# The silu-up product kept in the PSUM bank of up: a mixture-of-experts feed-forward with a mask product on VectorE

## The chip, the cores and the metric

The kernel runs on one core of a Trainium2 chip. The metric is the device time of one execution in microseconds. The engines are named TensorE (PE), VectorE (DVE), ScalarE (ACT), GpSimd (POOL) and SyncE (SP); PEld is TensorE's weight load.

## What is computed

Two layers of a gated transformer run one after the other on x, 4 sequences of 512 tokens with 128 features (2048 tokens in all). Each layer adds a gated cross-attention term (in layer 0 an alignment by dynamic time warping, in layer 1 an attention with 16 heads) and then a gated feed-forward term. The change touches only the feed-forwards. Cut to what matters, they are

```python
# layer 0: 64 experts of width 64, the 8 best by sigmoid score; one shared expert
expert_act = silu(gate_out) * up_out                       # per token and expert
routed = einsum(expert_act * router_mask[..., None], expert_down_k)
# layer 1: 8 experts of width 344, the 2 best by softmax; one shared expert
y = y + cw[:, e:e+1] * (silu(xf @ wg[e].T) * (xf @ wu[e].T)) @ wd[e].T
```

All experts are computed for all tokens; the routing weight, zero where a token did not choose the expert, is multiplied in as a mask before the down projection.

## The kernel before, in words

Tokens stand in the free dimension: xn_hi and xn_lo hold the normalised x transposed, 128 features by 2048 tokens, split into a rounded high part and the low rest, because TensorE multiplies in a reduced fp32 format. A product of two split operands takes three matmuls (`three_pass`, L1010 to L1014: high by high, low by high, high by low).

The hidden units of all experts, the shared one included, are cut into groups of 128: 33 groups in feed-forward 0 and 25 in feed-forward 1. The 2048 tokens are cut into four chunks of 512. A **unit** is one group on one chunk, u = 4g + k; there are 132 and 100 of them, 232 in all. Per unit:

- TensorE, `gate_up` (L1128 to L1139): three matmuls of 512 columns for gate into PSUM bank 4 + k % 2, three for up into bank 6 + k % 2. Then `down` (L1141 to L1148) of unit u - 2: two matmuls with the high part of the masked product (L1144, L1145), and a third (L1147), which waits for its low part. They add up in banks 0 to 3, one per chunk, over all groups.
- ScalarE, `unit` (L836 to L848): act_s = silu(gate) (L846); then `hi` (L829 to L834) of unit u - 1, which rounds act_a to act_hi.
- VectorE, `unit` (L1629 to L1648): L1639 multiplies act_s by the up bank into act_t, L1647 multiplies act_t by the mask into act_a.
- GpSimd, `unit` (L695 to L701): L700 subtracts, act_lo = act_a - act_hi.
- Once per group, at chunk 2, ScalarE rounds the next group's weights (L842) and VectorE computes their low part (L1626), 128 by 384 each, both in SBUF.
- SyncE's queue reloads a half of the weight buffer (L477, L480; L489 in feed-forward 1) when the group that used it is done with it, and a half of the mask buffer (L486; L500), a megabyte per group written to 128 partitions, when `act` says that the last product of the group two before is through.

Every tile between the engines has two halves, taken in turn by k % 2, and each step waits on counting semaphores: `gate`, `up`, `silu`, `t` (L1639 done), `act` (L1647 done), `ahi`, `alo`, `down`. Each engine works through its list in order. The waits that the change touches are on TensorE, before the gate of unit u:

```python
pe.wait_ge(FF[f]["silu"], u - 1)
pe.wait_ge(FF[f]["t"], u - 1)
```

A wait for the value u - 1 means that unit u - 2 has passed that step. ScalarE also waits for `t` of u - 2 before it writes act_s again.

The first 3 groups and the last 2 are written out; between them runs a hardware loop on each engine over 4 groups (16 units) per turn, 7 turns in feed-forward 0 and 5 in feed-forward 1. In the first units of feed-forward 0, VectorE also does the top-8 routing, in those of feed-forward 1 the top-2 routing, each step placed by hand in front of a unit (`ROUTE1_BEFORE`). After the last unit the sums are copied to yT, transposed back into banks 4 to 7 and added to x (`close`, `back`, `add_ffn`).

SBUF tiles of stages that do not overlap share one `arena`; the trace shows mask, act_s, act_t, act_a, yT and xT all by that name, and every PSUM bank as `bank`.

Of the kernel before, what the change touches and what calls it, by code (L numbers as in the profile page):

```python
# [29 lines left out]
P = 128  # L30
# [6 lines left out]
def program(nc, x, ctx_1024, g_xattn, g_ffn, r0_w, sg0, su0, sd0, eg0, eu0, ed0,  # L37
# [23 lines left out]
    CHUNKS = TOK // 512  # L61
# [17 lines left out]
    FT = -(-FLAT // P)  # L79
# [18 lines left out]
    with ctx:  # L98
# [6 lines left out]
        ps = [ctx.enter_context(nc.psum_tensor(f"bank{i}", [P, 512], F32)) for i in range(8)]  # L105
# [69 lines left out]
        mark = [0]  # L175
# [46 lines left out]
        mark[0] = 0  # L222
        mask = view([2, TOK])
        act_s = view([2, 512])
        act_t = view([2, 512])
        act_a = view([2, 512])
        yT = view([CHUNKS, 512])
        mark[0] += FT * P
        XT_FROM = mark[0]
        xT = view([TOK])  # L230
        aff = [view([TILES, E]) for E in EXPERTS]
# [699 lines left out]
        def _(pe):  # L931
# [52 lines left out]
            for g in range(GROUPS[1]):  # L984
                j = g % 2
# [24 lines left out]
            def three_pass(out, w_h, w_l, x_h, x_l, start=True, stop=True):  # L1010

                nc.tensor.matmul(out, w_h, x_h, start=start, stop=False)  # L1012
                nc.tensor.matmul(out, w_l, x_h, start=False, stop=False)  # L1013
                return nc.tensor.matmul(out, w_h, x_l, start=False, stop=stop)  # L1014
# [110 lines left out]
            def feed_forward(f):  # L1125
                units = CHUNKS * GROUPS[f]

                def gate_up(g, k, j):  # L1128
                    u = CHUNKS * g + k
                    if k == 0:  # L1130
                        pe.wait_ge(FF[f]["wlo"], g + 1)
                    if not (isinstance(g, int) and u < 2):
                        pe.wait_ge(FF[f]["silu"], u - 1)
                        pe.wait_ge(FF[f]["t"], u - 1)
                    tok = slice(512 * k, 512 * (k + 1))
                    three_pass(ps[4 + k % 2][:], w_hi[:, j, 0:P], w_lo[:, j, 0:P],
                               xn_hi[:, tok], xn_lo[:, tok]).then_inc(FF[f]["gate"], 1)
                    three_pass(ps[6 + k % 2][:], w_hi[:, j, UP:UP + P], w_lo[:, j, UP:UP + P],
                               xn_hi[:, tok], xn_lo[:, tok]).then_inc(FF[f]["up"], 1)  # L1139

# [30 lines left out]
                for n in range(CHUNKS):  # L1171

                    nc.tensor.matmul(ps[n][:], zeros[0:1, 0:P], zeros[0:1, :], start=True, stop=False)
                for u in range(2, CHUNKS * PEEL):
                    gate_up(u // CHUNKS, u % CHUNKS, u // CHUNKS % 2)
                    down(u - 2, (u - 2) % CHUNKS, (u - 2) // CHUNKS % 2)
                with pe.Fori(0, LOOPS[f]) as t:
# [13 lines left out]
                def back(n):  # L1191

                    if n == 0:
                        pe.wait_ge(FF[f]["silu"], units)
                    if n == 2:
                        pe.wait_ge(FF[f]["t"], units)
                    pe.wait_ge(FF[f]["yT"], n + 1)
                    for q in range(4):
                        mm = nc.tensor.transpose(ps[4 + n][:, P * q:P * (q + 1)], yT[:, n, P * q:P * (q + 1)], ident[:])
                    mm.then_inc(FF[f]["back"], 1)  # L1200
# [18 lines left out]
        def _(dve):  # L1219
# [402 lines left out]
            def feed_forward(f):  # L1622
# [6 lines left out]
                def unit(g, k, j, half, last=False):  # L1629
# [4 lines left out]
                        split_lo(g + 1, 1 - j)  # L1634
                    dve.wait_ge(FF[f]["silu"], u + 1)
                    dve.wait_ge(FF[f]["up"], u + 1)
                    if not early:
                        dve.wait_ge(FF[f]["act"], u - 1)
                    nc.vector.tensor_tensor(act_t[:, i, :], act_s[:, i, :], ps[6 + i][:], ALU.mult).then_inc(FF[f]["t"], 1)  # L1639
                    if f == 0 and isinstance(g, int) and g == 1:  # L1640
                        dve.wait_ge(s_mask1[k], 16 * MASK_DMAS)
                    elif k == 0:
# [1 line left out]
                    dve.wait_ge(FF[f]["t"], u + 1)  # L1644
                    if not early:
                        dve.wait_ge(FF[f]["alo"], u - 1)
                    nc.vector.tensor_tensor(act_a[:, i, :], act_t[:, i, :], mask[:, j, 512 * k:512 * (k + 1)],  # L1647
                                            ALU.mult).then_inc(FF[f]["act"], 1)  # L1648

                for g in range(PEEL):  # L1650
# [57 lines left out]
```

## Time and profile before

| | |
|---|---|
| runs (us) | 926.32, 926.35, 929.34; median 926.35 |
| profiled execution: span from first to last instruction (us) | 928.2 |
| profiled execution: own time | not listed apart from the runs |
| instructions | 13152 |
| busy, share of the span | PE 77%, VectorE 83%, ScalarE 47%, GpSimd 47% |
| mean granted TensorE clock | 0.868 of full |
| feed-forward 0, first gate after the opening to the last unit's gate (us) | 228.3 to 535.7 |
| feed-forward 1, the same (us) | 680.9 to 912.8 |

The span and the runs are measured in different executions. Busy time is the time in which an engine had an instruction under way; matmuls are pipelined, so one takes about 0.40 us while the next starts 0.23 us after it. The number behind an idle time in a row is what ended it. Instructions that wait for a port or a buffer inside the engine are shown as longer, not as idle.

### The profile page before, as it was taken

To read this page: it belongs to the slowest core of one execution; us is meant where nothing else is said; L and a number is where in the kernel's file an instruction comes from. 1 tells how busy PE (TensorE), PEld (TensorE's weight loads), DVE (VectorE), ACT (ScalarE), POOL (GpSimd) and SP (SyncE) were. 2 spreads that over 40 slices of the span, in tenths; PEclk is the share of its full clock that TensorE was granted. 3 is DMA by queue.
4 is the path that set the end of the run, shared out by engine and by line. 5 is a ranking of instruction groups with operands and counts; after the bars stand their busy time and mean duration, and the time that the engine had idled before them with its cause. 6 is when DMAs were issued, how large, how long until landed. Compare 5 with 4: busy or idle time off the path is not lost.

```text
span 928.2 us, 13152 instructions
## 1 busy us (share of the span) xinstructions
PE 714.0 (77%) x3115; PEld 537.3 (58%) x3115; DVE 773.9 (83%) x1829; ACT 432.5 (47%) x757; POOL 438.0 (47%) x451
## 2 busy tenths in 40 slices
PE   3422200038999999999999978999999999999996
PEld 2211100036776676767667647998866767766674
DVE  6599569998899898989889887777697988989895
ACT  2344100024555555555555545444445555555553
POOL 5568600005655556565555652110136565555653
PEclk9655555555999999999999978999589999999999
DMA  4454650003676675757666400000327656455551
GB/s 122 78 127 137 146 65 0 0 9 75 147 146 124 131 137 124 140 113 146 121 136 132 116 1 9 1 0 0 72 53 147 145 114 147 117 142 127 129 131 46
DMA packets 84164, 89.44 MB, mean 96 GB/s; under 512 B 48958, under 2 KB 61859, under 8 KB 80609
## 3 DMA queue, kind: packets, MB, share of 16 engines
q1 hardware_dynamic: 79808, 79.38, 41.3%
q0 software_dynamic: 4320, 9.68, 3.7%
q8 instruction: 11, 0.18, 0.1%
q14 instruction: 25, 0.20, 0.1%
HBM read 79.84 MB, written 8.70 MB: 95 GB/s over the span
## 4 chain that ended last, share of the span: by engine, by line
DVE 27%; issue 27%; PE 25%; POOL 11%; ACT 5%; DMA 3%; SPq 1%; POOLq 1%; DVEq 0%
POOL act_lo L700 10%; DVE arena L1647 8%; DVE junk L1417 6%; PE bank L1012 4%; PE bank L1076 4%; PE bank L1014 4%; PE bank L1013 4%; ACT act_hi L834 3%; PE bank L1147 2%; PE bank L1058 2%; DVE arena L1374 2%; DVE arena L1383 1%; PE bank L948 1%; DVE arena L1639 1%; PE bank L1144 1%
## 5 line engine op out<-in xcount | busy, mean ns | idle before, releaser
L700 POOL TENSOR_TENSOR act_lo<-arena,act_hi 128x512 fp32r<-128x512 f32 x232 | 323.4, 1403 | 237.7 <-ACT act_hi L834 232.1
L1647 DVE TENSOR_TENSOR arena<-arena 128x512 f32<-128x512 f32 x232 | 311.2, 1341 | 22.1 <-POOL act_lo L700 12.3
L846 ACT ACTIVATE arena<-bank 128x512 f32<-128x512 f32 x232 | 138.9, 599 | 140.7 <-PE bank L1014 137.2
L834 ACT ACTIVATE act_hi<-arena 128x512 fp32r<-128x512 f32 x232 | 147.0, 633 | 94.2 <-PE bank L1147 51.0
L1012 PE MATMUL bank<-xn_hi,w_hi 128*128 128x512 f32 x464 | 188.4, 406 | 3.1 <-issue 1.9
L1639 DVE TENSOR_TENSOR arena<-arena,bank 128x512 f32<-128x512 f32 x232 | 157.8, 680 | 37.1 <-ACT arena L846 19.6
L1013 PE MATMUL bank<-xn_hi,w_lo 128*128 128x512 f32 x464 | 185.6, 400 | 0.0
L1014 PE MATMUL bank<-xn_lo,w_hi 128*128 128x512 f32 x464 | 185.6, 400 | 0.0
L1147 PE MATMUL bank<-act_lo,w_hi 128*128 128x512 f32 x232 | 104.1, 449 | 31.2 <-POOL act_lo L700 30.9
L1012 PEld LDWEIGHTS bank<-xn_hi,w_hi 128*128 128x128 f32 x464 | 88.7, 191 | 26.8 <-issue 7.2
L1014 PEld LDWEIGHTS bank<-xn_lo,w_hi 128*128 128x128 f32 x464 | 88.5, 191 | 21.1
L1013 PEld LDWEIGHTS bank<-xn_hi,w_lo 128*128 128x128 f32 x464 | 88.5, 191 | 18.9
L1144 PE MATMUL bank<-act_hi,w_hi 128*128 128x512 f32 x232 | 92.6, 399 | 0.0
L1145 PE MATMUL bank<-act_hi,w_lo 128*128 128x512 f32 x232 | 91.8, 396 | 0.0
L1147 PEld LDWEIGHTS bank<-act_lo,w_hi 128*128 128x128 f32 x232 | 43.6, 188 | 83.2 <-POOL act_lo L700 77.8
L602 POOL TENSOR_SCALAR xn<-x_res,mv,rstd 128x128 f32<-128x128 f32 x16 | 13.8, 866 | 135.9 <-DVE rstd L1307 106.8
L992 PE MATMUL bank<-ident,prep_in 128*128 128x128 f32 x75 | 22.1, 431 | 64.8 <-DMA prep_in<-in_L_ffn_wd 57.7
L1417 DVE TENSOR_SCALAR_CACHE_REDUCE junk<-arena,ecol 4x511 f16<-4x511 f16 x76 | 56.5, 744 | 8.3 <-DMA arena<-arena 5.6
L1000 PE MATMUL bank<-ident,ecol 128*77 128x128 f32 x1 | 0.5, 499 | 77.7 <-DVE junk L1417 77.7
L992 PEld LDWEIGHTS bank<-ident,prep_in 128*128 128x128 f32 x75 | 12.4, 210 | 74.3 <-DMA prep_in<-in_L_ffn_wd 69.5
L1144 PEld LDWEIGHTS bank<-act_hi,w_hi 128*128 128x128 f32 x232 | 43.6, 188 | 11.4 <-issue 0.7
L1145 PEld LDWEIGHTS bank<-act_hi,w_lo 128*128 128x128 f32 x232 | 43.8, 189 | 10.2
(199 smaller groups left out, 956.2 us busy)
## 6 DMA issues: line engine op xcount, KB each, us to landing
arena<-scr_mask SPq DMA_DIRECT2D x94, 512.0 KB, 6.2
scr_w<-prep_out POOLq DMA_DIRECT2D x25, 192.0 KB, 2.2
w_raw<-scr_w SPq DMA_DIRECT2D x25, 192.0 KB, 6.5
arena<-scr_one SPq DMA_DIRECT2D x6, 512.0 KB, 6.0
w_raw<-in_L_ffn_expert_gate_k SPq DMA_DIRECT2D x32, 64.0 KB, 6.1
w_raw<-in_L_ffn_expert_up_k SPq DMA_DIRECT2D x32, 64.0 KB, 5.8
w_raw<-in_L_ffn_expert_down_k SPq DMA_DIRECT2D x64, 32.0 KB, 5.4
prep_in<-in_L_ffn_wg POOLq DMA_DIRECT2D x21, 64.0 KB, 2.4
```

Of the source, the lines that this page charges most:

```text
L700: nc.gpsimd.tensor_tensor(act_lo[:, k % 2, :], act_a[:, k % 2, :], act_hi[:, k % 2, :].bitcast(F32), ALU.subtract).then_inc(FF[f]["alo"], 1)
L834: nc.scalar.activation(act_hi[:, j, :], act_a[:, j, :], ACT.Copy).then_inc(FF[f]["ahi"], 1)
L846: nc.scalar.activation(act_s[:, k % 2, :], ps[4 + k % 2][:], ACT.Silu).then_inc(FF[f]["silu"], 1)
L1012: nc.tensor.matmul(out, w_h, x_h, start=start, stop=False)
L1013: nc.tensor.matmul(out, w_l, x_h, start=False, stop=False)
L1014: return nc.tensor.matmul(out, w_h, x_l, start=False, stop=stop)
L1144: nc.tensor.matmul(ps[n][:], w_hi[:, j, DOWN:DOWN + P], act_hi[:, i, :], start=False, stop=False)
L1145: nc.tensor.matmul(ps[n][:], w_lo[:, j, DOWN:DOWN + P], act_hi[:, i, :], start=False, stop=False)
L1147: nc.tensor.matmul(ps[n][:], w_hi[:, j, DOWN:DOWN + P], act_lo[:, i, :], start=False, stop=False).then_inc(FF[f]["down"], 1)
L1417: nc.vector.tensor_scalar(junk[CHASE, 1:S], chase[:, i, 1:S], ecol[CHASE, i:i + 1], 0.0, ALU.is_le, ALU.add, accum_out=ecol[CHASE, i - 1:i ...
L1639: nc.vector.tensor_tensor(act_t[:, i, :], act_s[:, i, :], ps[6 + i][:], ALU.mult).then_inc(FF[f]["t"], 1)
L1647: nc.vector.tensor_tensor(act_a[:, i, :], act_t[:, i, :], mask[:, j, 512 * k:512 * (k + 1)], ALU.mult).then_inc(FF[f]["act"], 1)
```

## The change

L1639 writes its product back into the PSUM bank that it reads up from, and L1647 reads it there. The tile act_t goes; the arena's later views keep their addresses from xT on, and act_a and yT move down. Since the bank of up is now in use until the mask product is done, TensorE's wait moves: before the gate it waits for `silu` only, and before up for `act` of unit u - 2 instead of `t`. VectorE's wait for its own `act` before L1639 goes. Units 2 and 3, which have none of these waits to stand for it, get a wait on xn_lo of their chunk (`wait_low`). The transposes at the end into bank 6 wait for the last `act` instead of the last `t`.

```diff
         act_s = view([2, 512])
-        act_t = view([2, 512])
         act_a = view([2, 512])
         yT = view([CHUNKS, 512])
-        mark[0] += FT * P
+        mark[0] += FT * P + 2 * 512
@@ TensorE, gate_up
                     if not (isinstance(g, int) and u < 2):
                         pe.wait_ge(FF[f]["silu"], u - 1)
-                        pe.wait_ge(FF[f]["t"], u - 1)
                     tok = slice(512 * k, 512 * (k + 1))
                     three_pass(ps[4 + k % 2][:], w_hi[:, j, 0:P], w_lo[:, j, 0:P],
                                xn_hi[:, tok], xn_lo[:, tok]).then_inc(FF[f]["gate"], 1)
+                    if not (isinstance(g, int) and u < 2):
+                        pe.wait_ge(FF[f]["act"], u - 1)
                     three_pass(ps[6 + k % 2][:], w_hi[:, j, UP:UP + P], w_lo[:, j, UP:UP + P],
                                xn_hi[:, tok], xn_lo[:, tok]).then_inc(FF[f]["up"], 1)
@@ TensorE, feed_forward
                 for u in range(2, CHUNKS * PEEL):
+                    if u < CHUNKS:
+                        wait_low(pe, 2 * f + 1, u)
                     gate_up(u // CHUNKS, u % CHUNKS, u // CHUNKS % 2)
@@ TensorE, back
                     if n == 2:
-                        pe.wait_ge(FF[f]["t"], units)
+                        pe.wait_ge(FF[f]["act"], units)
@@ VectorE, unit
                     dve.wait_ge(FF[f]["up"], u + 1)
-                    if not early:
-                        dve.wait_ge(FF[f]["act"], u - 1)
-                    nc.vector.tensor_tensor(act_t[:, i, :], act_s[:, i, :], ps[6 + i][:], ALU.mult).then_inc(FF[f]["t"], 1)
+                    nc.vector.tensor_tensor(ps[6 + i][:], act_s[:, i, :], ps[6 + i][:], ALU.mult).then_inc(FF[f]["t"], 1)
...
-                    nc.vector.tensor_tensor(act_a[:, i, :], act_t[:, i, :], mask[:, j, 512 * k:512 * (k + 1)],
+                    nc.vector.tensor_tensor(act_a[:, i, :], ps[6 + i][:], mask[:, j, 512 * k:512 * (k + 1)],
                                             ALU.mult).then_inc(FF[f]["act"], 1)
```

## Rows read from the trace of the kernel before

**Rows 1.** Costliest groups: line, engine, operation, count | busy us, mean ns | idle before, releaser

```profile
L1647 DVE TENSOR_TENSOR arena<-arena 128x512 f32<-128x512 f32 x232 | 311.2, 1341 | 22.1 <-POOL act_lo L700 12.3
```

**Rows 2.** Timeline in the loop of feed-forward 0: start us, duration us, engine, line

```profile
343.47 1.29 POOL L700 TENSOR_TENSOR act_lo<-arena,act_hi 128x512 fp32r<-128x512 f32 x1 [1.37 <-ACT act_hi L834]
...
343.61 1.71 DVE L1647 TENSOR_TENSOR arena<-arena 128x512 f32<-128x512 f32 x1
...
348.53 0.69 DVE L1647 TENSOR_TENSOR arena<-arena 128x512 f32<-128x512 f32 x1
```

**Rows 3.** Windows: stretch, length, busy PE, PEld, DVE, ACT, POOL, clock, DMA, GB/s

```profile
263.90:529.30 265.40, 249.70 (x1006) 184.36 (x1005) 238.31 (x252) 149.75 (x251) 154.59 (x112) 1.00 0.65 132
709.00:905.00 196.00, 184.40 (x745) 136.62 (x744) 176.33 (x186) 111.21 (x186) 114.12 (x83) 1.00 0.58 132
```

**Rows 4.** Waits in 263.9 to 529.3: total us, times, longest us

```profile
PE bank L1147 <- POOL act_lo L700: 14.6, 28, 0.6
```

**Rows 5.** Timeline of TensorE, two units at pace and one loop edge

```profile
360.28 0.39 PE L1012 MATMUL bank<-xn_hi,w_hi 128*128 128x512 f32 x1
...
364.48 0.40 PE L1012 MATMUL bank<-xn_hi,w_hi 128*128 128x512 f32 x1
...
366.43 0.50 PE L1147 MATMUL bank<-act_lo,w_hi 128*128 128x512 f32 x1
367.11 0.47 PE L1012 MATMUL bank<-xn_hi,w_hi 128*128 128x512 f32 x1 [0.18 <-issue]
367.42 0.40 PE L1013 MATMUL bank<-xn_hi,w_lo 128*128 128x512 f32 x1
```

**Rows 6.** Timeline: first gate matmul of units 2, 4, 131; then units 11, 99

```profile
228.31 0.47 PE L1012 MATMUL bank<-xn_hi,w_hi 128*128 128x512 f32 x1 [0.85 <-DVE arena L1639]
...
234.52 0.39 PE L1012 MATMUL bank<-xn_hi,w_hi 128*128 128x512 f32 x1
...
535.69 0.40 PE L1012 MATMUL bank<-xn_hi,w_hi 128*128 128x512 f32 x1
...
704.14 0.40 PE L1012 MATMUL bank<-xn_hi,w_hi 128*128 128x512 f32 x1
...
912.83 0.39 PE L1012 MATMUL bank<-xn_hi,w_hi 128*128 128x512 f32 x1
```

**Rows 7.** Timeline ahead of feed-forward 0, VectorE beside GpSimd

```profile
210.55 0.74 DVE L1265 SCALAR_TENSOR_TENSOR x_res<-bank,tgate,x_res 128x512 f32<-128x512 f32 x1
210.62 1.26 POOL L608 TENSOR_TENSOR xn_lo<-arena,xn_hi 128x512 fp32r<-128x512 f32 x1
```

**Rows 8.** Timeline in the loop: steps of one unit, and a rounding with its subtraction

```profile
341.24 0.39 PE L1012 MATMUL bank<-xn_hi,w_hi 128*128 128x512 f32 x1
...
342.13 0.60 ACT L846 ACTIVATE arena<-bank 128x512 f32<-128x512 f32 x1 [1.62 <-PE bank L1014]
...
342.88 0.69 DVE L1639 TENSOR_TENSOR arena<-arena,bank 128x512 f32<-128x512 f32 x1 [0.24 <-PE bank L1014]
...
345.35 0.63 ACT L834 ACTIVATE act_hi<-arena 128x512 fp32r<-128x512 f32 x1 [0.52 <-DVE arena L1647]
...
346.06 1.29 POOL L700 TENSOR_TENSOR act_lo<-arena,act_hi 128x512 fp32r<-128x512 f32 x1 [1.29 <-ACT act_hi L834]
```

**Rows 9.** One line's instructions: count, duration ns min/median/max

```profile
L1626 DVE TENSOR_TENSOR w_lo<-w_raw,w_hi x54: 543/546/1544, 240.5 to 903.1; 128x384 fp32r<-128x384 f32 x54
...
L1639 DVE TENSOR_TENSOR arena<-arena,bank x232: 628/678/689, 227.5 to 914.5; 128x512 f32<-128x512 f32 x116
```

**Rows 10.** Timeline, the mask product of unit 8 in feed-forward 1

```profile
700.61 0.69 DVE L1647 TENSOR_TENSOR arena<-arena 128x512 f32<-128x512 f32 x1 [2.28 <-DMA arena<-scr_mask]
```

**Rows 11.** Timeline, the last mask product of feed-forward 0

```profile
538.07 1.68 DVE L1647 TENSOR_TENSOR arena<-arena 128x512 f32<-128x512 f32 x1
```

**Rows 12.** Issue of two mask transfers, and DMA share in 339.8 to 349.3 (40 slices)

```profile
339.87 1.45 SPq L486 DMA_DIRECT2D arena<-scr_mask  x2
...
DMA  0000005599998995969597899999999998510000
```

## The prediction

> **What bounds the kernel now.** I read the page's costliest groups first, then two long windows over the feed-forward loops, the list of waits in the first of them, and single units in the timeline. The mask product (L1647) has both inputs in SBUF and takes 1341 ns on average [rows 1]. The average hides two kinds of instruction. With GpSimd quiet the mask product takes 0.69 us; started 0.14 us behind a GpSimd subtraction of 1.29 us it takes 1.71 us, ending 0.56 us after that subtraction does: the two do not share, one stands still [rows 2]. The windows say who else is near a limit: in the two loops TensorE is busy 94%, VectorE 90%, ScalarE 56%, GpSimd 58%, with the clock granted in full (2.4 GHz, shown as 1.00) [rows 3]. So TensorE is nearly the bound, but not quite: in 265 us it stands idle 14.6 us before the third down matmul for GpSimd's low half [rows 4], and the matmul that restarts is late as well.
>
> What TensorE needs by itself: two whole units (nine matmuls each) start 4.20 us apart where nothing holds them, so 2.10 us a unit [rows 5]. What a unit takes: in the first feed-forward, the gate of unit 2 starts at 228.31 and that of unit 131 at 535.69, 307.4 us for 129 units or 2.38 us each; in the second, unit 11 at 704.14 and unit 99 at 912.83, 208.7 us for 88 units, 2.37 us each [rows 6]. The 0.27 us between is what the change can reach, some 60 us at most.
>
> **Removed: the second SBUF operand of L1647.** The product will read PSUM and one SBUF tensor. Does that set it free of GpSimd? The trace has such a pair: L1265 reads a PSUM bank and x_res (SBUF) and takes 0.74 us at 210.55, while a GpSimd subtraction with two SBUF inputs runs from 210.62 for 1.26 us. Neither is stretched [rows 7]. So I take 0.69 us for the mask product in every unit and 1.29 us for L700. The Trainium skill, page "SBUF — State Buffer", section "Who interferes with whom", says that a VectorE instruction with one SBUF input at most uses only its own ports, and that one with two excludes a GpSimd instruction that reads SBUF for the whole of it; [rows 2, 7] agree.
>
> **Added: the PSUM output of L1639.** No VectorE instruction of this trace writes PSUM. Today the instruction takes 0.69 us [rows 8]. Lower bound 0.63 us, the shortest of its own 232 [rows 9]; a gain beyond that is excluded, as 512 columns still pass. Upper bound: reads and writes of the one bank take turns. A column costs 1.1 ns (0.69 us for 512 columns [rows 2], 0.546 us for the 384 of L1626 [rows 9]), so a second pass adds 0.58 us: 1.27 us. I take 0.69, nearest to the same instruction with the same inputs, and keep 1.27 for the range.
> By the Trainium skill, page "VectorE: DVE Perf Modes", section "The TRN2 errata", a PSUM source costs 120 cycles fixed and an SBUF source 58, which would make the mask product dearer by an estimated 0.06 us and the gain in each tail (below) smaller by as much; the rows differ from it (0.69 us with a PSUM input, 0.69 without), and the measurement decides.
>
> **Does the chain of one unit then fit in TensorE's pace?** Time 0 is the first gate matmul of unit u. Its silu starts at 0.89 and ends at 1.49; L1639 starts at 1.64 (both [rows 8]), ends 2.33; the mask product follows to 3.07. ScalarE's silu of u+1 runs 2.99 to 3.59, so the rounding (L834, 0.63 us) starts at 3.60 and ends 4.23; L700 follows it by 0.08 [rows 8] and runs 4.31 to 5.60. TensorE wants the low half for its ninth matmul of slot u+2, at 4.20 + 8 x 0.233 = 6.06, its weight load 0.2 earlier. Slack 0.2 to 0.4 us. The mask product has 0.5 us before ScalarE asks. Once per four units L1626 (two SBUF inputs, 0.55 us) still meets GpSimd: it arrives at about 1.0 of its slot, L700 of two units before holds until 1.4, so L1639 starts 0.3 us late and the mask product ends near 3.4, still before 3.60. So TensorE sets the pace.
>
> **Moved: waits.** The gate loses its wait on t(u-2), free in the steady state. The up product gains a wait on act(u-2), reached 3.07 us after that unit's start and asked for at 4.90: 1.8 us of cover. Behind it on TensorE's queue stand up, down and the next gate; if the cover goes they all slip. VectorE loses a wait on its own earlier result, worth nothing; xn_lo waits for units 2 and 3 are for work long finished; back(2) now waits for the last act, which its own sums need anyway. SBUF addresses move, with no transfer changed. All nil.
>
> **The sum.** First feed-forward: 129 x 2.10 = 270.9, plus loop edges. At an edge the starts are 0.68 and 0.31 us apart instead of 0.233 twice, so 0.52 us [rows 5]; entry, six returns and exit make 8 x 0.52 = 4.2. The two first units took 6.21 us (228.31 to 234.52 [rows 6]) with a slow clock, 2.0 over pace, kept. Together 277.1 against 307.4: 30.3 us. Second, from unit 11: 88 x 2.10 + 6 x 0.52 = 187.9 against 208.7: 20.8 us. Its first nine units gain little, since unit 8 waits for a mask from memory until 700.61 [rows 10], which routing and stores set: 0.5 us, for the blocking just behind it. Each tail ends with a mask product stretched to 1.68 us [rows 11], 1.0 us shorter, with nothing beside it: 2.0 us. In all 53.6 us. Everything outside the feed-forwards is as before. The span of 928.2 becomes 874.6; the profiled execution's own time is not listed apart from the three runs, whose median of 926.35 lies 1.9 us under its span. On the median: 872.8, so 873.
>
> **Rivals.**
> 1. VectorE becomes the bound. If L1639 takes 1.27 us, one group of four units costs it 4 x (0.71 + 0.61 + 0.58) + 0.46 = 8.1 us (starts are some 0.08 apart less than durations), plus L1626 waiting for GpSimd, up to 1.3; TensorE needs 8.4. At a wait of 0.6 the group is 8.7, 0.07 us a unit, 226 units: 16 us given back, 889. At the whole wait, 9.4: 926 less a few. For it: in-place use of one bank is nowhere in the trace. Against: mixed operands cost nothing so far. Chance 0.12.
> 2. Masks come late. A half of the mask buffer is reloaded once its group's last product is done; what is issued from 339.87 on (two mask transfers, then four of weights) has left the DMA engines by 348.4 [rows 12], 8.5 us. Reload, then the four products of the group (3 x 2.10 + 0.69 = 7.0) give a cycle of 15.6 us with the 0.16 to issue, against 16.8 for two groups at the new pace. 1.2 us of cover are left, of more than 3 today. If denser traffic stretches the load by 2.5 us, the cycle is 18.1, or 2.26 a unit: 36 us given back, 909; by 1.5, 10 us, 883. Chance 0.08, mostly the smaller.
> 3. The change does not do what it says: the SBUF tensor as second input is still fetched by the way shared with GpSimd. Then all stays, 926. [Rows 7] has just this order of operands, free. Chance 0.03.
> 4. Slower: VectorE's in-place pass and the blocking both stand, so the pair of products grows. Today's group is 9.5 us; the case decides once L1639 and L1647 together exceed some 2.3 us from start to start, when up's new wait on act holds TensorE's whole queue. With 1.27 and 1.34 us the group is 4 x 2.54 + 0.46 = 10.6, 0.28 us a unit more than now: 926 + 63 = 989. Chance 0.02.
>
> **How the numbers follow.** The forecast has 0.72; the remaining 0.03 is for gains spoilt by a start or a clock that I did not see (0.02 faster, 0.01 slower). Two ends of measurement: below, edges and the start could vanish too, 6 us, so 866. Above, rivals 1 and 2 in their likelier form: 891. That leaves out rivals 3, 4 and the tails of 1 and 2. A measurement of this kernel tells about 0.5% (4.6 us) from no change. Faster 0.94, same 0.03, slower 0.03.
>
> **What would show it.** Right: L1647 at 0.69 us in nearly all 232, L700 at 1.29 throughout, VectorE busy in the loops down from 90% to about 70%, gate starts 2.10 us apart in both loops, no wait of TensorE for L700 beyond the edges, and L1626 the only VectorE instruction of the loops still stretched. Wrong: L1639 over 1 us (rival 1); VectorE waiting at L1647 for scr_mask in the loops (rival 2); L1647 still in two kinds (rival 3); TensorE waiting at the up product for L1647 (rival 4), or a granted clock under 1.00 in the loops now that TensorE has no pauses.

## The result, and the profile after

The changed kernel ran in 863.47, 863.52, 865.79 and 867.64 us, median 864.65, against 926.48 (926.32 to 929.34, four runs) before: a ratio of 0.9327, 95% interval 0.9301 to 0.9353. That is 61.8 us less; the prediction had 53.6 less, 873.0, and its range ended at 866, 1.35 us above the median. The direction and the mechanism came as forecast, the size was too small. Four executions on record, three of the kernel before and one of e6, took 1421 to 3168 us, and the medians below leave them out.

The profiled execution after took 865.79 us with a span of 864.1; the clock granted on average is 0.865 (0.868 before). From span to span 64.1 us went. The line numbers of the engines' units have moved by one or two: L699 is the old L700, L833 the old L834, L1011 to L1013 the old L1012 to L1014, L1628 the old L1626; L1639 and L1647 keep theirs.

The page of the kernel after: engine totals, some of the costliest groups (line engine operation out<-in, count | busy us, mean ns of one | idle us before them, what ended it) and the chain that ended last by engine.

```profile
PE 679.6 (79%) x3115; PEld 542.2 (63%) x3115; DVE 646.6 (75%) x1829; ACT 412.3 (48%) x757; POOL 414.4 (48%) x451
...
PE 69%; DVE 20%; issue 4%; DMA 3%; ACT 2%; POOL 1%; SPq 1%; DVEq 0%; POOLq 0%; ACTq 0%
...
L699 POOL TENSOR_TENSOR act_lo<-arena,act_hi 128x512 fp32r<-128x512 f32 x232 | 300.3, 1294 | 200.6 <-ACT act_hi L833 200.6
L1639 DVE TENSOR_TENSOR bank<-arena,bank 128x512 f32<-128x512 f32 x232 | 160.7, 693 | 105.9 <-PE bank L1013 73.5
...
L1647 DVE TENSOR_TENSOR arena<-bank,arena 128x512 f32<-128x512 f32 x232 | 160.5, 692 | 19.8 <-DVE bank L1639 9.2
...
L1147 PE MATMUL bank<-act_lo,w_hi 128*128 128x512 f32 x232 | 92.7, 400 | 2.0 <-POOL act_lo L699 2.0
```

GpSimd's subtraction in the kernel before, from the same list of its page:

```profile
L700 POOL TENSOR_TENSOR act_lo<-arena,act_hi 128x512 fp32r<-128x512 f32 x232 | 323.4, 1403 | 237.7 <-ACT act_hi L834 232.1
```

The mask product stood at 311.2 us [rows 1]; it now stands at 160.5, 692 ns each. L1639 takes nearly the same time although it writes PSUM. GpSimd's subtraction went from 1403 ns on average to 1294: where the mask product started first, it had been the subtraction that was stretched. TensorE waits 2.0 us in all for the low half, where it stood 14.6 us in one window alone [rows 4]. The chain that ended last runs over TensorE for 69% of the span.

Min, median and max of three lines' durations in ns, kernel after:

```profile
L1639 DVE TENSOR_TENSOR bank<-arena,bank x232: 666/696/697, 227.1 to 851.3; 128x512 f32<-128x512 f32 x116
...
L1647 DVE TENSOR_TENSOR arena<-bank,arena x232: 690/692/694, 227.8 to 852.0; 128x512 f32<-128x512 f32 x116
...
L1628 DVE TENSOR_TENSOR w_lo<-w_raw,w_hi x54: 742/880/1104, 239.7 to 840.1; 128x384 fp32r<-128x384 f32 x54
```

Not one of the 232 mask products is stretched: the spread is 4 ns. L1639 with its PSUM output takes 18 ns more (696 against 678 [rows 9]). Not all of that need be the output's: L1647, with one input in PSUM and the output in SBUF, takes 692. L1628, with both inputs in SBUF, is the one that still meets GpSimd: 0.74 to 1.10 us, where it needs 0.546 alone [rows 9].

Two windows over the loops (stretch, length, busy PE, PEld, DVE, ACT, POOL, clock, DMA share, GB/s), to be set beside [rows 3]:

```profile
263.90:497.30 233.40, 233.40 (x1003) 187.98 (x1002) 174.27 (x252) 139.00 (x250) 144.23 (x112) 1.00 0.74 149
672.00:849.00 177.00, 177.00 (x761) 142.57 (x761) 131.73 (x190) 105.30 (x191) 109.52 (x85) 1.00 0.63 143
```

TensorE is busy for all of it, VectorE for 75% instead of 90%, at a clock granted in full (2.4 GHz). The waits in the first window (engine line waited for: us in total, times, longest; the three largest) say the same from the other side; TensorE has no row, and VectorE now waits for TensorE's up product:

```profile
POOL act_lo L699 <- ACT act_hi L833: 89.9, 112, 0.9
ACT arena L845 <- PE bank L1013: 83.8, 98, 1.1
DVE bank L1639 <- PE bank L1013: 34.0, 58, 0.7
```

The timeline of the kernel after (start us, duration us): in feed-forward 0, the first gate matmul of unit 2, the first up matmul of unit 2 and the first gate matmuls of units 4 and 131; in feed-forward 1, the mask product of unit 8, which waited for the late mask, the first up matmul of unit 10, which waited for that product, and the gates of units 11 and 99. They answer to [rows 6, 10].

```profile
226.18 0.50 PE L1011 MATMUL bank<-xn_hi,w_hi 128*128 128x512 f32 x1
...
228.57 0.50 PE L1011 MATMUL bank<-xn_hi,w_hi 128*128 128x512 f32 x1 [1.43 <-DVE arena L1647]
...
234.57 0.39 PE L1011 MATMUL bank<-xn_hi,w_hi 128*128 128x512 f32 x1
...
500.97 0.39 PE L1011 MATMUL bank<-xn_hi,w_hi 128*128 128x512 f32 x1
...
661.95 0.69 DVE L1647 TENSOR_TENSOR arena<-bank,arena 128x512 f32<-128x512 f32 x1 [3.22 <-DMA arena<-scr_mask]
...
662.70 0.50 PE L1011 MATMUL bank<-xn_hi,w_hi 128*128 128x512 f32 x1 [1.27 <-DVE arena L1647]
...
665.06 0.40 PE L1011 MATMUL bank<-xn_hi,w_hi 128*128 128x512 f32 x1
...
849.64 0.40 PE L1011 MATMUL bank<-xn_hi,w_hi 128*128 128x512 f32 x1
```

From such rows comes the ledger (us, of the two profiled executions; "charged" is what the prediction's sum had for the stretch):

| stretch | before | after | saved | charged |
|---|---|---|---|---|
| start to gate of unit 4, feed-forward 0 | 234.5 | 234.6 | -0.1 | 0 |
| units 4 to 131, 127 units | 301.2 | 266.4 | 34.8 | 30.3 |
| to gate of unit 2, feed-forward 1 | 145.2 | 140.8 | 4.4 | 1.0 |
| units 2 to 11 | 23.3 | 23.3 | 0.0 | 0.5 |
| units 11 to 99, 88 units | 208.7 | 184.6 | 24.1 | 20.8 |
| unit 99 to the end | 15.4 | 14.4 | 1.0 | 1.0 |
| sum | 928.2 | 864.1 | 64.1 | 53.6 |

(The rows are rounded one by one.) The difference of 10.5 us has three places: 4.5 and 3.3 in the loops, and 3.4 between the feed-forwards; 0.6 goes off again at the two openings. In the medians it is 8.2 us, since the profiled execution of before was a long one, its span alone 1.7 us over the median of the runs.

In the loops after, 127 units take 266.4 us and 88 take 184.6: 2.098 us each in both, loop edges included. So the edges, charged with 0.52 us each [rows 5], cost nothing. Here is TensorE across the edge before unit 60, timeline of the kernel after:

```profile
351.81 0.40 PE L1147 MATMUL bank<-act_lo,w_hi 128*128 128x512 f32 x1
352.05 0.39 PE L1011 MATMUL bank<-xn_hi,w_hi 128*128 128x512 f32 x1
352.28 0.39 PE L1012 MATMUL bank<-xn_hi,w_lo 128*128 128x512 f32 x1
```

The starts are 0.24 and 0.23 us apart, as anywhere inside the body; in the kernel before they were 0.68 and 0.31 [rows 5].

### The profile page after: what moved, and what is told of

It reads as the page before. It is cut to its first block, busy times and chain, and to the rows that moved or that the text cites. A ratio compares the mean times of both kernels' runs of the same rounds, so it can differ in the third digit from the quotient of the medians.

```text
span 864.1 us, 12936 instructions
## 1 busy us (share of the span) xinstructions
PE 679.6 (79%) x3115; PEld 542.2 (63%) x3115; DVE 646.6 (75%) x1829; ACT 412.3 (48%) x757; POOL 414.4 (48%) x451
## 4 chain that ended last, share of the span: by engine, by line
PE 69%; DVE 20%; issue 4%; DMA 3%; ACT 2%; POOL 1%; SPq 1%; DVEq 0%; POOLq 0%; ACTq 0%
PE bank L1011 14%; PE bank L1012 13%; PE bank L1013 13%; DVE junk L1419 7%; PE bank L1147 6%; PE bank L1144 6%; PE bank L1145 6%; PE bank L1075 4%; PE bank L1057 2%; DVE arena L1376 2%; DVE arena L1385 1%; PE bank L947 1%; DVE arena L1384 1%; DMA arena<-scr_d 1%; DVE arena L1386 1%
## 5 line engine op out<-in xcount | busy, mean ns | idle before, releaser
L699 POOL TENSOR_TENSOR act_lo<-arena,act_hi 128x512 fp32r<-128x512 f32 x232 | 300.3, 1294 | 200.6 <-ACT act_hi L833 200.6
L1639 DVE TENSOR_TENSOR bank<-arena,bank 128x512 f32<-128x512 f32 x232 | 160.7, 693 | 105.9 <-PE bank L1013 73.5
L1011 PE MATMUL bank<-xn_hi,w_hi 128*128 128x512 f32 x464 | 185.9, 401 | 3.0 <-DVE arena L1647 3.0
L1012 PE MATMUL bank<-xn_hi,w_lo 128*128 128x512 f32 x464 | 185.7, 400 | 0.0
L1013 PE MATMUL bank<-xn_lo,w_hi 128*128 128x512 f32 x464 | 185.0, 399 | 0.0
L1647 DVE TENSOR_TENSOR arena<-bank,arena 128x512 f32<-128x512 f32 x232 | 160.5, 692 | 19.8 <-DVE bank L1639 9.2
L833 ACT ACTIVATE act_hi<-arena 128x512 fp32r<-128x512 f32 x232 | 145.3, 626 | 12.8 <-DVE arena L1647 12.8
L1011 PEld LDWEIGHTS bank<-xn_hi,w_hi 128*128 128x128 f32 x464 | 88.3, 190 | 26.3 <-DVE arena L1647 4.3
L1013 PEld LDWEIGHTS bank<-xn_lo,w_hi 128*128 128x128 f32 x464 | 88.4, 191 | 21.2
L1012 PEld LDWEIGHTS bank<-xn_hi,w_lo 128*128 128x128 f32 x464 | 88.3, 190 | 20.8
L1147 PE MATMUL bank<-act_lo,w_hi 128*128 128x512 f32 x232 | 92.7, 400 | 2.0 <-POOL act_lo L699 2.0
```

The costliest lines, as they stand in the source:

```text
L699: nc.gpsimd.tensor_tensor(act_lo[:, k % 2, :], act_a[:, k % 2, :], act_hi[:, k % 2, :].bitcast(F32), ALU.subtract).then_inc(FF[f]["alo"], 1)
L833: nc.scalar.activation(act_hi[:, j, :], act_a[:, j, :], ACT.Copy).then_inc(FF[f]["ahi"], 1)
L1147: nc.tensor.matmul(ps[n][:], w_hi[:, j, DOWN:DOWN + P], act_lo[:, i, :], start=False, stop=False).then_inc(FF[f]["down"], 1)
L1639: nc.vector.tensor_tensor(ps[6 + i][:], act_s[:, i, :], ps[6 + i][:], ALU.mult).then_inc(FF[f]["t"], 1)
L1647: nc.vector.tensor_tensor(act_a[:, i, :], ps[6 + i][:], mask[:, j, 512 * k:512 * (k + 1)], ALU.mult).then_inc(FF[f]["act"], 1)
```

## The experiments

Three theories had to be told apart. **A**: VectorE's second SBUF input excludes GpSimd's instruction, and its removal is the whole gain. **B**: part of the gain is from the moved waits, which let TensorE take gates earlier. **C**: part of it is that an edge costs a fixed time that vanished with something else. The runs are told in the order of these questions.

### The moved waits alone

`e1_waits_only` is the kernel before with TensorE's waits as in the change; the product stays in SBUF.

```diff
-                        pe.wait_ge(FF[f]["t"], u - 1)
                     three_pass(ps[4 + k % 2][:], ...).then_inc(FF[f]["gate"], 1)
+                    if not (isinstance(g, int) and u < 2):
+                        pe.wait_ge(FF[f]["act"], u - 1)
...
                 for u in range(2, CHUNKS * PEEL):
+                    if u < CHUNKS:
+                        wait_low(pe, 2 * f + 1, u)
```

> The kernel before with the moved waits alone: act_t stays in SBUF, TensorE's gate waits for silu only and up waits for act of u - 2. Theory A (the gain is the end of the mutual blocking of L1647 and GpSimd's L700): 923 to 932 us, L1647 in two kinds again (0.69 and 1.5 to 1.7 us), a unit in the loops at 2.38 us. Rival B (the gain comes from the gate no longer waiting for VectorE): under 905 us with L1647 still stretched. Where act_t is reused early, ScalarE's and VectorE's own order still keeps it apart, so nothing of the computation is left out.

Measured: 928.62 us (eight runs, 925.7 to 932.01) against 926.24, ratio 1.0018, interval 0.9992 to 1.0043. Four units still take 9.51 us. Its mask product, durations in ns (min, median, max):

```profile
L1650 DVE TENSOR_TENSOR arena<-arena x232: 691/1490/1801, 227.0 to 915.9; 128x512 f32<-128x512 f32 x116
```

Two kinds of instruction, as before. The waits bring nothing that can be measured: B falls for the loops.

`e2_wait_ahead_of_gate` is the changed kernel with its new wait put ahead of the gate, behind the one for `silu`.

```diff
                         pe.wait_ge(FF[f]["silu"], u - 1)
+                        pe.wait_ge(FF[f]["act"], u - 1)
                     three_pass(ps[4 + k % 2][:], ...).then_inc(FF[f]["gate"], 1)
-                    if not (isinstance(g, int) and u < 2):
-                        pe.wait_ge(FF[f]["act"], u - 1)
```

> The changed kernel with the wait for act of u - 2 put ahead of the gate instead of ahead of up, where the wait for t stood. Theory A: act of u - 2 comes about 3.1 us after that unit's start and the gate asks at 4.20, so the loops keep 2.10 us a unit; 862 to 869 us, the opening of each feed-forward up to 2 us different. Rival B (placing the wait between gate and up matters): over 875 us.

Measured: 867.57 (866.71 to 868.21), ratio 0.9363, interval 0.9349 to 0.9378, with 8.39 us for four units in both loops, as in the changed kernel. At the new pace the product is through before the gate is due, so in the loops it doesn't matter where the wait stands. Behind the late mask of feed-forward 1 it does. The first gate matmul of unit 10, timeline of e2:

```profile
662.99 0.47 PE L1011 MATMUL bank<-xn_hi,w_hi 128*128 128x512 f32 x1 [2.26 <-DVE arena L1646]
```

In the changed kernel that gate started without a wait and only up waited. From the gate of unit 0 to that of unit 11 it takes 31.2 us here, 29.7 in the changed kernel: the place of the wait is worth 1.5 us, once.

`e4_first_gates_wait` keeps the change and holds back only the gates of units 2 and 3, which the change had let start earlier (226.18 for unit 2, against 228.31 [rows 6]).

```diff
                         pe.wait_ge(FF[f]["silu"], u - 1)
+                        if isinstance(g, int) and u < 4:
+                            pe.wait_ge(FF[f]["act"], u - 1)
```

> The changed kernel in which the gates of units 2 and 3 also wait for act of u - 2. In the profile of the changed kernel gate 2 of feed-forward 0 starts 2.1 us earlier than before, but units 2 and 3 take 8.4 us instead of 6.2, with the granted clock at half for longer. Theory C (the early gate only moves TensorE's pause to where it costs clock): gate 4 comes at the same 234.5 us or up to 2 us earlier, total 861 to 867 us. Rival (the start is set by VectorE's and GpSimd's routing and the clock falls anyway): gate 4 later by 1 to 2 us, 865 to 868 us.

Measured: 866.08 (863.99 to 867.86), ratio 0.9352, interval 0.9338 to 0.9366. Unit 2 starts at 227.55 here and unit 4 at 233.37; counted from unit 0's own gate, unit 4 comes after 14.0 us here and 14.1 in the changed kernel, so the later start is no loss. In the changed kernel the up product of unit 2 waits 1.43 us for the mask product of unit 0, and unit 4 stands where it stood before: the 2.1 us won at unit 2 are given back at once.

### The order of operands

`e3_mask_first` swaps the two inputs of the mask product; the masked product is the same.

```diff
-                    nc.vector.tensor_tensor(act_a[:, i, :], ps[6 + i][:], mask[...],
+                    nc.vector.tensor_tensor(act_a[:, i, :], mask[...], ps[6 + i][:],
                                             ALU.mult).then_inc(FF[f]["act"], 1)
```

> The changed kernel with the operands of L1647 exchanged: the mask (SBUF) is the first input, the PSUM bank the second. Theory A (what counts is how many inputs lie in SBUF): no change, 862 to 869 us, L1647 0.69 us throughout. Rival (one of the two input places is shared with GpSimd whatever lies there): L1647 or L700 stretched in many of 232 and over 900 us.

Measured: 865.93 (862.64 to 868.69), ratio 0.9347, interval 0.9319 to 0.9374. The line's durations:

```profile
L1647 DVE TENSOR_TENSOR arena<-arena,bank x232: 686/687/690, 227.7 to 851.5; 128x512 f32<-128x512 f32 x116
```

One SBUF input is free in either place; it is the count of SBUF inputs that matters.

### An instruction added: mixed, both in SBUF, both in SBUF but earlier

Three kernels add one VectorE product per unit to the changed kernel. Each writes act_t, which nobody reads and which gets its tile back, so the outputs stay. They differ in the inputs and the place.

```diff
+                    # e7: ahead of the mask product, PSUM and SBUF
+                    nc.vector.tensor_tensor(act_t[:, i, :], ps[6 + i][:], mask[...], ALU.mult)
+                    # e8: at the same place, SBUF twice
+                    nc.vector.tensor_tensor(act_t[:, i, :], mask[...], mask[...], ALU.mult)
+                    # e9: ahead of L1639, SBUF twice
+                    nc.vector.tensor_tensor(act_t[:, i, :], act_s[:, i, :], act_s[:, i, :], ALU.mult)
```

> The changed kernel with one more VectorE product per unit, between L1639 and L1647: PSUM bank times mask into an unused SBUF tile, so one input in PSUM and one in SBUF. VectorE then has three products a unit: 4 x 1.92 + 0.46 = 8.1 us a group by the starts, plus its wait for GpSimd at L1628, against TensorE's 8.39. Theory: near the edge of its cover, 0 to 0.1 us a unit lost: 865 to 888 us, no L699 stretched by the new product. Rival (VectorE's work, not blocking, was the bound before): three products a unit give at least the time of before, 926 us or more.

> The same as the run with the extra mixed product, but the extra product has both inputs in SBUF (mask times mask), at the same place, at some 2.35 us after the unit's first gate matmul, where L699 of the unit before holds from 2.2 to 3.5. Theory: it is blocked until L699 is done and in turn holds up the next; at least 1.3 instead of 0.69 us for it, 4 x 2.55 + 0.46 = 10.7 us a group, 2.66 us a unit, about 990 us (range 950 to 1030). Rival (an extra instruction costs the same wherever its inputs lie): the time of the run with the mixed product, within 5 us.

> The changed kernel with an extra product with both inputs in SBUF (act_s times act_s) ahead of L1639 instead of behind it, so from 1.64 to 2.3 us after the unit's first gate matmul. L699 of two units before is done at 1.4 and that of the unit before starts at 2.2. Theory (what counts is which instructions overlap in time): it falls between two of GpSimd's and costs as the mixed one does, 865 to 895 us. Rival (any product with two SBUF inputs costs the blocking, wherever it stands): as the run with it behind L1639, 950 us or more.

| | median us (runs) | ratio, interval | 16 units in the loop, us |
|---|---|---|---|
| changed kernel | 864.65 | 0.9327, 0.9301 to 0.9353 | 33.56 |
| e7, mixed | 879.27 (876.88 to 882.18) | 0.9482, 0.9446 to 0.9518 | 34.25 |
| e8, both SBUF | 991.51 (989.18 to 993.46) | 1.0698, 1.067 to 1.0725 | 42.55 |
| e9, both SBUF, early | 884.21 (881.73 to 885.8) | 0.9531, 0.95 to 0.9563 | 34.54 |

The costliest groups of e7, the subtraction (here L700) and the added line:

```profile
L700 POOL TENSOR_TENSOR act_lo<-arena,act_hi 128x512 fp32r<-128x512 f32 x232 | 301.1, 1298 | 214.0 <-ACT act_hi L834 169.7 <-PE bank L1148 44.3
...
L1648 DVE TENSOR_TENSOR arena<-bank,arena 128x512 f32<-128x512 f32 x232 | 160.5, 692 | 19.2 <-DVE bank L1640 9.2 <-DMA arena<-scr_mask 2.9
```

The same of e8:

```profile
L700 POOL TENSOR_TENSOR act_lo<-arena,act_hi 128x512 fp32r<-128x512 f32 x232 | 351.6, 1516 | 272.4 <-ACT act_hi L834 272.4
...
L1648 DVE TENSOR_TENSOR arena<-arena 128x512 f32<-128x512 f32 x232 | 252.6, 1089 | 17.6 <-DVE bank L1640 9.2 <-DMA arena<-scr_mask 1.4
```

And of e9:

```profile
L700 POOL TENSOR_TENSOR act_lo<-arena,act_hi 128x512 fp32r<-128x512 f32 x232 | 313.3, 1351 | 204.6 <-ACT act_hi L834 171.7 <-PE bank L1148 32.9
...
L1640 DVE TENSOR_TENSOR arena<-arena 128x512 f32<-128x512 f32 x232 | 161.0, 694 | 6.3 <-ACT arena L846 3.0 <-PE bank L1014 1.8
```

e7 and e8 issue the same number of VectorE instructions of the same size at the same place. The mixed one costs 14.6 us, the other 126.9. Between e7 and e8 only the source of one input is changed, and the subtraction goes from 1298 to 1516 ns, the added product from 692 to 1089. The timeline of e8 shows both orders of arrival:

```profile
380.36 1.27 POOL L700 TENSOR_TENSOR act_lo<-arena,act_hi 128x512 fp32r<-128x512 f32 x1 [1.89 <-ACT act_hi L834]
...
380.72 1.46 DVE L1648 TENSOR_TENSOR arena<-arena 128x512 f32<-128x512 f32 x1
...
383.42 0.69 DVE L1648 TENSOR_TENSOR arena<-arena 128x512 f32<-128x512 f32 x1
383.53 1.72 POOL L700 TENSOR_TENSOR act_lo<-arena,act_hi 128x512 fp32r<-128x512 f32 x1 [1.89 <-ACT act_hi L834]
```

In the first pair GpSimd is first: it takes 1.27 us and VectorE, started 0.36 behind it, ends at 382.18, 0.55 after GpSimd's end at 381.63. In the second pair VectorE is first, takes 0.69 and ends at 384.11; GpSimd ends at 385.25, 1.14 later. Whoever comes first is untouched; of the other's work nearly all follows (0.55 of 0.69 us, 1.14 of 1.27). The rest of the trace is alike: 110 of the 232 added products are stretched behind GpSimd, 117 start first and stretch GpSimd. This is A, seen from both sides; no run here tells GpSimd's reads from its write. The Trainium skill, page "SBUF — State Buffer", section "Who interferes with whom", says that the order of issue decides who is blocked; the two pairs agree.

e9 adds to it. Its product also has both inputs in SBUF, yet it takes 694 ns on average and costs 19.6 us in all, not 127: ahead of L1639 half of the 232 overlap no subtraction, two are stretched themselves, and 56 start first, so that GpSimd waits (1351 ns on average). So what costs is two SBUF inputs at the time of GpSimd's instruction, not two SBUF inputs as such. VectorE's added work is not free either: e7, whose added product is never stretched (691 to 694 ns), loses 0.69 us a turn of 16 units, 10 us over 14.5 turns, because VectorE has become the bound (busy 226.0 of 236.1 us between 263.9 and 500, with 0.5 us of waits for other engines); the rest of its loss lies outside the loops.

### The loop edges

`e5_before_fewer_edges` is the kernel before with 19 groups written out instead of 3, so that 16 groups of each feed-forward have no edge; SyncE's loop stays as it was.

```diff
-    PEEL, BODY, REST = 3, 4, 2
+    PEEL, BODY, REST = 19, 4, 2
...
-            with sp.Fori(0, (GROUPS[0] - PEEL) // 2) as t:
+            with sp.Fori(0, (GROUPS[0] - 3) // 2) as t:
...
-                    g, j = 2 * t + PEEL + jj, 1 - jj
+                    g, j = 2 * t + 3 + jj, 1 - jj
```

> The kernel before with 19 groups written out instead of 3, so that each hardware loop has four turns fewer (3 instead of 7, and 1 instead of 5): 8 loop edges of 14 are gone. The prediction charged 0.52 us to each. If edges add to the time: 8 x 0.52 = 4 us less, about 922 us, and units in the written-out part faster than in the loop. If they are absorbed (the gate starts of before show 9.51 us per group with an edge in it as without): 924 to 930 us, 9.51 us per group throughout.

Measured: 923.73 (twelve runs) against 927.74, ratio 0.9956, interval 0.9935 to 0.9976. Gates of units 12, 72, 92 and 108 in feed-forward 0, timeline of e5; the first two lie in the written-out part, the last two at loop edges:

```profile
251.44 0.39 PE L1012 MATMUL bank<-xn_hi,w_hi 128*128 128x512 f32 x1
...
392.94 0.40 PE L1012 MATMUL bank<-xn_hi,w_hi 128*128 128x512 f32 x1
...
440.83 0.47 PE L1012 MATMUL bank<-xn_hi,w_hi 128*128 128x512 f32 x1 [0.21 <-issue]
...
478.92 0.47 PE L1012 MATMUL bank<-xn_hi,w_hi 128*128 128x512 f32 x1 [0.19 <-issue]
```

Written out, 15 groups take 141.50 us, 9.43 each; in the loop, four groups take 38.09, 9.52 each. The difference is 0.09 per group, not 0.52 per edge, and the groups around an edge show why: in the kernel before they take 9.86 and then 9.19, 19.05 together, twice the 9.52 of any other. TensorE starts late behind the edge and has caught up one group later, because VectorE set the pace and TensorE had 4 x (2.38 - 2.10) = 1.1 us per group to spare. The small rest, 32 groups by 0.09, 2.9 us, is within what the medians show (4.0, interval 2.2 to 6.0); it is spread over the whole loop, and its cause stays open. The medians alone would fit 8 edges at 0.52 us, 4.2, just as well; it is the group times that rule this out, and C with it. The expectation for absorbed edges (9.51 us throughout, 924 to 930) was missed by this rest.

`e6_after_fewer_edges` makes the same edit in the changed kernel.

> The changed kernel with 19 groups written out instead of 3: 8 of 14 loop edges are gone. Theory (an edge behind a filled queue costs nothing): 862 to 868 us, 8.39 us a group in the written-out part and in the loop, with an edge in it or without. Rival (each edge costs 0.52 us): about 4 us less, 860 to 861 us, and written-out groups faster than the average of the loop.

Measured: 866.78 (five runs, 864.85 to 867.97), ratio 0.934, interval 0.9314 to 0.9366. Every group takes 8.39 us, in the written-out part and in the loop. With this TensorE-bound body an edge costs nothing.

Why is it late before and not after? `e10_drain_at_edge` and `e11_drain_in_body` make TensorE wait for its own last down matmul once per turn, the one just ahead of the branch, the other in the middle of the body.

```diff
                             down(CHUNKS * g + k - 2, (k + 2) % CHUNKS, j if k >= 2 else 1 - j)
+                            if i == BODY - 1 and k == CHUNKS - 1:   # e11: i == 1
+                                pe.wait_ge(FF[f]["down"], CHUNKS * g + k - 1)
```

> The changed kernel with one more wait on TensorE at the end of every loop turn, right ahead of the branch: for the down product just issued, so that its queue is empty when the branch comes. Theory (an edge is free because TensorE's instructions are queued ahead of the matmuls, and costs only where the queue is empty): each of 12 turns loses the drain and the restart (0.4 to 0.6 us, as in the run with the same wait inside the body) and 0.2 to 0.5 us for the branch on top, 872 to 877 us. Rival (edges are free in any case): the same time as the run with the wait inside the body, within 1 us.

> The changed kernel with the same extra wait, but in the middle of every loop turn (after its eighth unit). It gives the price of an emptied queue without a branch: 12 x 0.4 to 0.6 us, 869 to 872 us. Where it differs from the run with the wait at the end of the turn, the difference is the branch.

Measured: e10 877.61 (873.66 to 880.97), ratio 0.9462, interval 0.9425 to 0.9499; e11 872.56 (869.34 to 876.26), 0.9404, 0.9367 to 0.9441; both medians lie 0.6 us above what was expected. The last matmul ahead of the wait and the first behind it, timeline of e10:

```profile
282.73 0.40 PE L1147 MATMUL bank<-act_lo,w_hi 128*128 128x512 f32 x1
283.83 0.50 PE L1011 MATMUL bank<-xn_hi,w_hi 128*128 128x512 f32 x1 [0.71 <-PE bank L1147]
```

The same of e11:

```profile
269.26 0.39 PE L1147 MATMUL bank<-act_lo,w_hi 128*128 128x512 f32 x1
269.88 0.50 PE L1011 MATMUL bank<-xn_hi,w_hi 128*128 128x512 f32 x1 [0.23 <-PE bank L1147]
```

The starts are 1.10 us apart with the wait at the branch and 0.62 with it in the body, 0.233 without a wait. Sixteen units take 34.45 and 34.05 us, so the branch costs 0.40 us more per turn when TensorE has stopped just ahead of it; 12 turns make 4.8, and the medians are 5.05 apart.

In the kernel before, the last down matmul ahead of the edge starts at 366.43 with 0.50 us [rows 5], late, after a wait for the low half. That happens at every group boundary, with a branch or without. Timeline of the kernel before across a boundary inside the turn, before unit 56:

```profile
356.92 0.50 PE L1147 MATMUL bank<-act_lo,w_hi 128*128 128x512 f32 x1
357.26 0.43 PE L1012 MATMUL bank<-xn_hi,w_hi 128*128 128x512 f32 x1
357.53 0.40 PE L1013 MATMUL bank<-xn_hi,w_lo 128*128 128x512 f32 x1
```

Here the starts are 0.34 and 0.27 us apart, at the edge 0.68 and 0.31. So the branch's own share of the delay is 0.38 us, near the 0.40 of e10 against e11, and the rest follows any such stall. In the kernel after nothing waits there, and the branch is taken while matmuls are still under way.

e9, in which the low half comes only just in time again, has the delay back, with TensorE busy 235.5 of 236.1 us. Timeline of e9 at the same edge, before unit 60:

```profile
357.24 0.19 PEld L1148 LDWEIGHTS bank<-act_lo,w_hi 128*128 128x128 f32 x1 [0.21 <-POOL act_lo L700]
...
357.31 0.43 PE L1148 MATMUL bank<-act_lo,w_hi 128*128 128x512 f32 x1
...
357.82 0.50 PE L1012 MATMUL bank<-xn_hi,w_hi 128*128 128x512 f32 x1
```

The starts are 0.51 us apart, and the two groups around an edge take 8.80 and 8.64 us where the others take 8.55, so here each turn really loses 0.35. An edge is free where TensorE runs well ahead of its waits, as in the changed kernel, and not simply because TensorE sets the pace. What happens inside TensorE's queue at a branch no trace here shows.

## Why the prediction was right, and where it was wrong

**The lock.** Right, in all its steps: the mask product at 0.69 us in all 232 units, GpSimd's subtraction at 1.29, only the weights' low part still stretched. e1, e3, e7 and e8 show that it is one SBUF input instead of two that does it. Rival 3 is out.

**The price of the PSUM output.** Right: 696 ns where 690 was taken and 1270 kept as the upper end. Rival 1 is out: taking turns would have shown as 1270. The 0.06 us more for a PSUM source, which the prediction set aside, does not show either: 692 ns for the mask product, against 691 for the shortest one with both inputs in SBUF (e1).

**The chain of one unit.** Right within 0.05 us. Unit 59 begins at 349.95: L1639 started 1.67 us later (1.64 in the prediction), L1647 at 2.40 (2.38), the subtraction at 4.26 (4.31).

```profile
349.95 0.40 PE L1011 MATMUL bank<-xn_hi,w_hi 128*128 128x512 f32 x1
...
351.62 0.70 DVE L1639 TENSOR_TENSOR bank<-arena,bank 128x512 f32<-128x512 f32 x1 [0.64 <-PE bank L1013]
...
352.35 0.69 DVE L1647 TENSOR_TENSOR arena<-bank,arena 128x512 f32<-128x512 f32 x1
...
354.21 1.29 POOL L699 TENSOR_TENSOR act_lo<-arena,act_hi 128x512 fp32r<-128x512 f32 x1 [0.88 <-ACT act_hi L833]
```

VectorE was busy 75% of the loops, not 70; the pace came out at 2.098 against 2.10. No load of a mask was late in the loops (rival 2 is out), and the fourth rival's place, up waiting for `act`, shows only in the opening and behind the late mask. The granted clock is 1.00 in both loops.

**The moved waits.** Right in the loops: nil (e1, e2). The wait on `act` did bite twice, 1.43 us at unit 2 and 1.27 us at unit 10 of feed-forward 1, both times where something else set the time. The 0.5 us that the sum had for units 2 to 11 is not in the ledger's row, though 0.4 of it came: from the start of unit 8's mask product to the gate of unit 11 it takes 3.1 us instead of 3.5. The mask itself comes 26.6 us after unit 0's gate, in the kernel before 26.5, and unit 2, at which the row begins, starts 0.4 us earlier on that count.

**The tails.** Feed-forward 1's is 1.0 us shorter, as charged. Feed-forward 0's last mask product takes 0.69 instead of 1.68 [rows 11].

**The loop edges.** Here the prediction was wrong: "At an edge the starts are 0.68 and 0.31 us apart instead of 0.233 twice, so 0.52 us", and from it 8 edges, then 6, at 0.52 us, 7.3 us kept for the kernel after. They cost nothing (e6): this is the step that failed, a term of 7.3 us that measured 0. Three things were passed over. A late start behind an edge is a cost only if the groups around it take longer, and the rows of before, read two groups wide, say that they don't. The delay shows only behind a stall, the very one that the change removes; it was carried over as if the branch always had it. And one edge stood for all 14: in the kernel before only the ten returns show 0.68 to 0.73 us, while at the two entries and two exits the starts are 0.24 to 0.41 us apart. The range had this case in it, but only with 6 us, which from 872.8 makes 866.8 and was written as 866; the 7.3 us of its own sum would have put the end at 865.5. Without the edges, and with 2.098 for 2.10, the same sum gives 61.3 us and 865.0, against a measured 864.65. That it comes so close is in part luck, as the next item shows; e2, e3, e4 and e6, which keep the pace, have ratios of 0.934 to 0.936, which is 865 to 868 us against the same 926.48.

**Between the feed-forwards.** "Everything outside the feed-forwards is as before" is the second term that was off, in the profiled execution: 3.4 us went here beyond what the tail explains. The clock granted to TensorE is in it. The windows of 2 us in which the clock falls after the loops of feed-forward 0, for the kernel before, the kernel after and e6 (columns as above):

```profile
652.00:654.00 2.00, 2.00 (x15) 2.00 (x15) 1.44 (x9) 1.85 (x6) 0.00 (x0) 0.70 0.00 0
```

```profile
622.00:624.00 2.00, 1.52 (x11) 0.98 (x10) 1.58 (x8) 0.89 (x2) 0.00 (x0) 0.83 0.00 0
```

```profile
614.00:616.00 2.00, 2.00 (x17) 2.00 (x17) 1.51 (x8) 1.99 (x6) 0.00 (x0) 0.83 0.00 0
```

Counted from unit 131's gate (535.69 and 500.97) the fall, from 1.00 to the lower level (1.2 GHz) within the window, comes after 117 us before and after 122 us in the changed kernel, so some 5 us more of this stretch run at 2.4 GHz. That this belongs to the change is not shown. From unit 131's gate to the first of feed-forward 1 it takes 138.4 us in the kernel before, 134.4 after. Of the other kernels whose code there is that of the changed one, e2, e3 and e4 have the fall after 121 to 122 us and take 134.0 to 134.4; e6, e10 and e11 have it after 116 to 118, as in the kernel before, and take 136.9 to 137.5, which leaves 0.9 to 1.5 us to the change, about the 1.0 of the tail. So some 3 us of the profiled execution go with the later fall, more than the 1.35 us by which the median passed the end of the range. What puts the fall early or late stays open; no run was made for it.

## What to carry to other kernels

Where VectorE and GpSimd work side by side, count the SBUF inputs of each VectorE instruction that overlaps a GpSimd instruction: give the second input a home in PSUM, or move the instruction to where GpSimd is quiet (e8 against e9: 107 us). Before an idle time at a loop edge is charged to the edge, read the period around it, and ask whether the stall ahead of it survives the change. A product written back into the PSUM bank that it reads is such a home at hardly a cost: 18 ns in 678 at most.

## What the hardware did that was not expected

- Writing the result over the PSUM bank that is being read costs VectorE at most 18 ns in 678 for 512 columns (696 in the changed kernel; the same product has a median of 683 in e8 and 687 in e9).
- VectorE with two SBUF inputs and GpSimd stretch each other, whoever comes second: 0.69 us becomes 1.46 to 1.71, 1.27 becomes 1.72 (e8, and the kernel before).
- The branch of a hardware loop is free for TensorE behind matmuls under way, and costs 0.40 us where TensorE has stopped just ahead of it (e10 against e11). Making TensorE wait for its own last matmul costs 0.39 us from start to start (0.62 instead of 0.233), 0.49 per turn.
- With VectorE as the bound, a group of four units takes 0.09 us more inside the hardware loop than written out (9.52 against 9.43); in the changed kernel, with TensorE as the bound, there is no difference (8.39 both).
